# Moving row moments from VectorE to ScalarE in a Mamba and linear-attention kernel, with a fourth x buffer and a reordered end

## What is computed

```
# block 1: conditional Mamba, state size N = 16, inner width 512
xn = layernorm(x) * (1 + scale) + shift          # scale, shift, gate from cond
x_in, z = split(xn @ in_proj.T)
u  = silu(causal_conv4(x_in) + conv_b)
dt_r, B, C = split(u @ x_proj.T);  dt = softplus(dt_r @ dt_proj.T + b)
h[t] = exp(dt[t] * A) * h[t-1] + dt[t] * u[t] * B[t]       # 512 x 16 states
y = (h . C + u * D) * silu(z)
x = x + gate * (y @ out_proj.T)
# block 2: linear attention, 8 heads of 32
xn = layernorm(x);  q = softmax(xn Wq, in a head);  k = softmax(xn Wk + mask, over rows)
v = (xn Wv) * mask;  y = q @ (k^T v)
x = x + silu(layernorm(y) * (1 + scale2) + shift2) @ W_out
```

## Time and profile before

| | us |
|---|---|
| median of 3 runs | 567.08 |
| lowest, highest | 566.95, 568.99 |
| the profiled execution, its own time | 567.71 |
| its span in the profile | 565.9 |

### The profile page before, as it was taken

The page is one execution under the profiler, slowest core; times in us unless marked ns, Lnnn a source line. Parts: engine busy times, 40 slices in busy tenths (PEclk is TensorE's granted clock), DMA queues, the critical chain, the costliest instruction groups (busy, mean ns, idle before and its releaser), DMA issues. The chain is left out here.

```text
span 565.9 us, 7375 instructions
## 1 busy us (share of the span) xinstructions
PE 437.7 (77%) x2448; PEld 361.3 (64%) x2448; DVE 515.5 (91%) x567; ACT 407.9 (72%) x896; POOL 452.8 (80%) x318
## 2 busy tenths in 40 slices
PE   8968656769787878859787688759787877766887
PEld 7647445557675767638675567647585766655776
DVE  2489999999999999999999999999999999999753
ACT  2693868588857989498947989489857988486533
POOL 4058979988997999978996989878996989995121
PEclk8978868888789899998879898999789798889899
DMA  8293043003320145012320045012330044000001
GB/s 255 80 346 109 0 151 113 37 28 107 103 92 0 30 158 161 1 29 87 139 94 1 28 152 167 1 30 78 124 118 1 10 152 167 2 0 20 0 1 37
DMA packets 22365, 45.37 MB, mean 80 GB/s; under 512 B 3684, under 2 KB 13556, under 8 KB 22328
## 3 DMA queue, kind: packets, MB, share of 16 engines
q1 hardware_dynamic: 22328, 44.92, 24.2%
HBM read 42.52 MB, written 2.39 MB: 79 GB/s over the span
## 5 line engine op out<-in xcount | busy, mean ns | idle before, releaser
L531 POOL TENSOR_TENSOR hs<-dtu,Br 128x1024 f32<-128x1024 f32 x127 | 296.8, 2359 | 7.9 <-DMA Br<-bc_rows 6.4
L726 ACT ACTIVATE ring<-dt,Aneg 128x256 f32<-128x256 f32 x512 | 212.9, 465 | 71.9 <-DVE hs L965 67.4
L958 DVE TENSOR_TENSOR_SCAN ring<-ring,hs 128x1024 f32<-128x1024 f32 x97 | 221.4, 2282 | 4.3 <-ACT ring L726 4.0
L1317 PE MATMUL sums<-ident,hs 128*128 128x128 f32 x1024 | 148.7, 301 | 37.8 <-DVE hs L965 37.7
L1317 PEld LDWEIGHTS sums<-ident,hs 128*128 128x128 f32 x1024 | 132.7, 157 | 49.0 <-DVE hs L965 45.5
L965 DVE TENSOR_TENSOR hs<-ring,Cr 128x1024 f32<-128x1024 f32 x97 | 118.7, 1224 | 3.3
L540 POOL TENSOR_TENSOR hs<-hs,Cr 128x1024 f32<-128x1024 f32 x31 | 73.1, 2357 | 39.8 <-DVE hs L958 39.8
L958 DVE TENSOR_TENSOR_SCAN hs<-ring,hs 128x1024 f32<-128x1024 f32 x31 | 70.3, 2268 | 0.0
L1385 PE MATMUL PY<-wqkvo,xT 128*128 128x256 f32 x168 | 49.8, 450 | 0.0
L1385 PEld LDWEIGHTS PY<-wqkvo,xT 128*128 128x128 f32 x168 | 39.9, 237 | 7.7
L616 ACT ACTIVATE conv<-PX,par 128x256 f32<-128x256 f32 x28 | 14.3, 559 | 38.2 <-PE PX L1251 38.0
(11 more groups left out here) (221 smaller groups left out, 693.6 us busy)
## 6 DMA issues: line engine op xcount, KB each, us to landing
Br<-bc_rows SPq DMA_DIRECT2D x32, 512.0 KB, 5.2
Cr<-bc_rows SPq DMA_DIRECT2D x32, 512.0 KB, 4.2
xg<-in_x SPq DMA_DIRECT2D x8, 256.0 KB, 2.9
out<-fin SPq DMA_DIRECT2D x7, 256.0 KB, 4.3
hs<-in_ada_wT SPq DMA_DIRECT2D x3, 512.0 KB, 5.2
win<-in_in_wT SPq DMA_DIRECT2D x2, 512.0 KB, 7.2
hs<-in_W_emb SPq DMA_DIRECT2D x2, 512.0 KB
gate<-gate_rows SPq DMA_DIRECT2D x8, 128.0 KB, 3.1
```

The costliest lines, as they stand in the source:

```text
L531: nc.gpsimd.tensor_tensor(hs[:, g % DBUF], dtu[:, b % 2, dc, :].unsqueeze(1).to_broadcast([P, NQ, T]), Br[:, NQ * q:NQ * q + NQ, :], ALU.m ...
L726: ins = nc.scalar.activation(ring[:, g % 2, j, :], dt[:, b % 2, dc, :], ACT.Exp, scale=Aneg[:, c:c + 1])
L958: V.tensor_tensor_scan(driven if by_pool(g) else decays, decays, driven, 0.0, ALU.mult, ALU.add).then_inc(s_scan_done, 1)
L1317: ins = M(YT[:, c, :], hs[:, g % DBUF, j, P * c:P * c + P], ident[:, :], is_transpose=True, start=False, stop=(q == UPC - 1 and j == NQ - ...
```

## The change

Five edits.
1. `moments` on ACT takes the place of `stats` on DVE for x of batches 2 to 7 and for the attention's rows of batches 0 to 5: two Copy ACTIVATEs with an accumulator (the negative mean), then, behind a wait for these, two Square ACTIVATEs with the bias from them (the sum of squared deviations). Their elementwise output goes into `xhat` or `xh` and is not used. POOL's `rstd` then has three operations instead of four for these.
2. `moments2` stands first among the steps behind unit 2, `moments0` last among those behind unit 3 (slot -29, four units ahead of where `stats0` stood).
3. `normalize2` moves from behind unit 6 to behind unit 4, POOL's `rstd2` by one unit.
4. XBUF is 4; x of batch 3 is loaded right behind x of batch 2 at the start, and each later load is that of one batch later, at the same place in SP's queue and behind the same wait.
5. The end: the last unit's product with C is made in two halves; `last_early` is split, its second half now ahead of unit 126's sums; ACT does `exp_k` of the last batch ahead of `normalize2` of batch 6, and the last `silu_h` ahead of `finish` of batch 6; PE's transposes of the last batch's rows come ahead of the addition of x1 for batch 6, and ten `keep_on` matmuls are gone.

```diff
-DBUF, XBUF = 10, 3
+DBUF, XBUF = 10, 4
+def moments_by_act(which, b):
+    return b >= 2 and which == 0 or b < LAST_B - 1 and which == 2
...
             load_x(2)
+            load_x(3)
...
-                if b + 2 < NB:
-                    load_x(b + 2)
+                if b + 3 < NB:
+                    load_x(b + 3)
...
+                if summed:
+                    nc.gpsimd.tensor_scalar(ve[:, :], mv[:, :, 1], 1.0 / D, EPS, ALU.mult, ALU.add).then_inc(ve_sem, 1)
...
+                if summed:
+                    nc.gpsimd.tensor_tensor(nb[:, :], mv[:, :, 0], rs[:, :], ALU.mult).then_inc(rs_sem, 1)
+                    return
...
-                                   (40, rstd2)):
+                                   (39, rstd2)):
...
+            def moments(b, src, junk, mv, ready):
+                for c in range(TC):
+                    nc.scalar.activation(junk[:, c, :], src[:, c, :], ACT.Copy, scale=-1.0 / D,
+                                         accum_out=mv[:, c, 0:1]).then_inc(ready, 1)
+                for c in range(TC):
+                    act.wait_ge(ready, 2 * TC * b + TC)
+                    nc.scalar.activation(junk[:, c, :], src[:, c, :], ACT.Square, bias=mv[:, c, 0:1],
+                                         accum_out=mv[:, c, 1:2]).then_inc(ready, 1)
+            def moments0(b):
+                if not moments_by_act(0, b):
+                    return
+                act.wait_ge(x_loaded[b % XBUF], 16 * (b // XBUF + 1))
+                act.wait_ge(s_xT_mm, b)
+                act.wait_ge(s_rs0_ready, 2 * b)
+                moments(b, xg[:, b % XBUF], xhat, mv0, s_st0_ready)
+            def moments2(b):
+                if not moments_by_act(2, b):
+                    return
+                act.wait_ge(s_yq_ready, b + 1)
+                act.wait_ge(s_x1T_mm, b + 1)
+                act.wait_ge(s_rs2_ready, 2 * b)
+                moments(b, yq, xh, mv2, s_st2_ready)
...
+                exp_k(LAST_B)
                 normalize2(LAST_B - 1)
-                exp_k(LAST_B)
...
+                silu_h(LAST_B)
                 finish(LAST_B - 1)
-                silu_h(LAST_B)
...
-                for slot, step in ((-17, normalize0), ...
+                for slot, step in ((34, moments2), (-17, normalize0), ...
-                                   (33, copy_kT), (38, normalize2), (42, finish)):
+                                   (33, copy_kT), (36, normalize2), (42, finish), (-29, moments0)):
...
+                if g == NB * U - 1:
+                    for half, done in ((slice(0, 2), s_last_half), (slice(2, NQ), s_hc_dve)):
+                        V.tensor_tensor(hs[:, g % DBUF, half], ring[:, g % 2, half], Cr[:, NQ * q:NQ * q + NQ, :][:, half],
+                                        ALU.mult).then_inc(done, 1)
+                    return
...
-                output(b - 1)
-                keep_on(4)
+                output_rows(b - 1)
                 pe.wait_ge(s_yh_ready, TC * b + 1)
                 turn_half(z, xhat, 0)
                 pe.wait_ge(s_yh_ready, TC * b + 2)
                 turn_half(z, xhat, 1).then_inc(s_yT_mm, 1)
+                output_x1(b - 1)
...
-                keep_on(6)
...
+                if g == LAST_B * U + 13:
+                    last_early(1)
                 if g == LAST_B * U + 14:
-                    last_early()
+                    last_early(0)
```

More of the change, by code:

```diff
@@ L477, in _, with rstd @@
             pool.wait_ge(s_pool_const, 8)
-            def rstd(ready, b, mv, ve, rs, nb, ve_sem, rs_sem, nbp_sem):
+            def rstd(which, ready, b, mv, ve, rs, nb, ve_sem, rs_sem, nbp_sem):
                 pool.wait_ge(ready, 2 * TC * (b + 1))
-                nc.gpsimd.tensor_scalar(ve[:, :], mv[:, :, 1], EPS, None, ALU.add).then_inc(ve_sem, 1)
+                summed = moments_by_act(which, b)
+                if summed:
+                    nc.gpsimd.tensor_scalar(ve[:, :], mv[:, :, 1], 1.0 / D, EPS, ALU.mult, ALU.add).then_inc(ve_sem, 1)
+                else:
+                    nc.gpsimd.tensor_scalar(ve[:, :], mv[:, :, 1], EPS, None, ALU.add).then_inc(ve_sem, 1)
                 pool.wait_ge(ve_sem, b + 1)
@@ L485, in rstd @@
                 pool.wait_ge(rs_sem, 2 * b + 1)
+                if summed:
+                    nc.gpsimd.tensor_tensor(nb[:, :], mv[:, :, 0], rs[:, :], ALU.mult).then_inc(rs_sem, 1)
+                    return
                 nc.gpsimd.tensor_tensor(nb[:, :], mv[:, :, 0], rs[:, :], ALU.mult).then_inc(nbp_sem, 1)
-                pool.wait_ge(nbp_sem, b + 1)
+                pool.wait_ge(nbp_sem, sum(not moments_by_act(which, c) for c in range(b + 1)))
                 nc.gpsimd.tensor_scalar(nb[:, :], nb[:, :], -1.0, None, ALU.mult).then_inc(rs_sem, 1)
@@ L492, in rstd0 @@
                     pool.wait_ge(s_xhat_ready, TC * b)
-                rstd(s_st0_ready, b, mv0, ve0, rs0, nb0, s_ve0_ready, s_rs0_ready, s_nbp0)
+                rstd(0, s_st0_ready, b, mv0, ve0, rs0, nb0, s_ve0_ready, s_rs0_ready, s_nbp0)
             def softplus_sum(b, h):
@@ L549, in rstd1 @@
                     pool.wait_ge(s_xh_ready, TC * b)
-                rstd(s_st1_ready, b, mv1, ve1, rs1, nb1, s_ve1_ready, s_rs1_ready, s_nbp1)
+                rstd(1, s_st1_ready, b, mv1, ve1, rs1, nb1, s_ve1_ready, s_rs1_ready, s_nbp1)
             def rstd2(b):
@@ L554, in rstd2 @@
                     pool.wait_ge(s_yh_ready, TC * b)
[L555 removed]
+                rstd(2, s_st2_ready, b, mv2, ve2, rs2, nb2, s_ve2_ready, s_rs2_ready, s_nbp2)
             for g in range(FIRST, LAST):
@@ L1315, in sum_states @@
                 for j in range(NQ):
+                    if g == NB * U - 1 and j == 2:
+                        pe.wait_ge(s_hc_dve, dve_units(g + 1))
                     for c in range(TC):
@@ L1359, in out_part, with last_early @@
                 return ins
-            def last_early():
+            def last_early(c):
                 pe.wait_ge(s_last_yg, 3)
-                for c in range(TC):
-                    out_part(c, (0, 1, 2))
+                out_part(c, (0, 1, 2))
             def out_half(dst, c):
```

15 lines of the change are left out of this document (13 added, 2 removed).

## The result

| | before | after |
|---|---|---|
| median of 4 runs each | 567.72 us (566.95 to 568.99) | 559.74 us (558.04 to 560.05) |
| profiled execution | 567.7 us, span 565.9 | 559.8 us, span 558.0 |
| mean granted clock of PE | 0.897 | 0.887 |

The ratio is 0.9852, 95% interval 0.9835 to 0.9869: 8.0 us less. 557.4 was forecast, with 554.5 to 562.0 as its range; it was reckoned from the 567.08 of the three runs known then, and from 567.72 the same 9.7 us would give 558.0. The change took 7.9 us from the span; the steps had promised 9.7.

The account below looks back on a forecast made before the run. DVE, busy 515.5 of 565.9 us, was taken as the bound, with ACT possibly late next. Gains of 4.8 + 3.5 - 0.6 + 2.0 = 9.7 us from the median of 567.1 gave 557.4 us, range 554.5 to 562.

Parts of the forecast that it names:

- The set on ACT: One set of moments on ACT, two Copies and two Squares: 2.0 us, between 1.8 and 2.6.
- DVE's busy time: Sign over the whole kernel: DVE busy 12 us less, about 503.5 us.
- A: Attention's moments moved from DVE to ACT, units 34 to 114: most of each 1.0 us set kept, 4.8 us gained.
- B: x's moments on ACT and normalize2 moved: 0.5 us at each of five places, 1.0 behind unit 23; 3.5 us gained.
- C: First moments0, behind unit 3, waits for x of batch 2 and delays the decays of unit 4: 0.6 us lost.
- D: The end: split product and last_early 0.15 us, exp_k first 0.75, last transposes ahead of x1's addition 1.1; 2.0 us gained.
- milder form of rival 1: PE's half clock falls elsewhere and delays ACT's convolution tap more often, at 0.2 to 0.5 us each.
- a new wait of DVE for PE: Sign named in advance: if such a wait appeared, the prediction would be wrong.
- Rival 1: ACT is late in most stretches, with a set of 2.6 us: 562.2 us; chance 0.2 for 560.5 to 564.
- Rival 2: Slower: a set keeps ACT over 3.2 us, where all 9.7 us are gone; 569.5 at 3.5; chance 0.04.
- Rival 3: The end keeps its time, PE falling to half clock without the ten dummies: 559.9 us; chance 0.07.
- Rival 4: No change within 0.5%: ACT's chain absorbs both sets and the end gives 2, about 565 us; chance 0.05.

Follow-up runs that it names:

- Run 8: The change with 16 spare PE matmuls per batch 2 to 7, every set of moments on ScalarE done twice: 575.59 us, ratio 1.0134.
- Run 1: The change with normalize2 put back to slot 38 and rstd2 to slot 40: 559.94 us, ratio 0.9861.
- run 6: The change with 16 spare PE matmuls per batch 2 to 7, x's moments on VectorE again, only the attention's on ScalarE: 558.92 us, ratio 0.9830.
- run 12: The change with 26 spare PE matmuls ahead of the sums of unit 6 in batches 2 to 7: 556.02 us, ratio 0.9787.
- run 3: The change with all moments of batches 0 to 7 on VectorE again, the rest kept: 569.05 us, ratio 1.0022.
- run 9: The change itself measured again, unaltered, on one chip beside later runs: 559.15 us, ratio 0.9829.
- run 2: The change with 16 spare PE matmuls ahead of the sums of unit 6 in batches 2 to 7: 556.89 us, ratio 0.9809.
- run 4: The change with the diff of the end reversed, so the old end: 559.27 us, ratio 0.9861.
- run 5: The kernel before with 16 spare PE matmuls ahead of the sums of unit 6 in batches 2 to 7: 568.14 us, ratio 1.0010.

## Why the prediction was right, and which terms were off

The direction, the mechanism and the size held: 559.7 us against 557.4, inside the range, though 2.3 us on the slow side. By its own steps:

- **The set on ACT** was sized at 2.0 us from `exp_k`'s row; it is 1.94: 0.40 us for each Copy, 0.50 for each Square and 0.12 for the wait between them. By the formula of the Trainium skill ("ScalarE: Activation LUTs", What ACT_TABLE_LOAD costs), with 0.1 us for each accumulator read, my estimate had been 1.8; the trace agrees with it to 0.01 us for each of the four, and only the wait was missing. (Run 8's added set, without wait and bias, takes 1.61 us.)
- **DVE's busy time** was forecast at 503.5 us and is 504.7.
- **A**, 4.8 us, came to 8.1. The steady steps are 0.94 us at unit 51 and 83 and 0.66 at 115 (0.9 or 0.65, and 0.7 forecast). The other three came to 1.37, 2.68 and 1.47, because in the kernel before ACT's tap had waited 6.51, 8.00 and 6.50 us for PE there, against 5.11 elsewhere, and DVE's taps had waited behind it for 0.33, 1.66 and 0.43 us. The largest, in the timeline of DVE before:

```profile
298.30 2.43 DVE L920 SCALAR_TENSOR_TENSOR conv<-PX,par,conv 128x255 f32<-128x255 f32 x6 [1.66 <-ACT conv L616]
```

  From 290 to 295 us the granted clock was 0.50 there. In the changed kernel ACT's tap waits for PE in none of these batches. I had taken the before profile's bad spots for fixed and priced them as a loss for the change ("0.65 kept"), where they were a gain.
- **B**, 3.5 us: 0.94 and 5 x 0.45 = 3.2. Run 1 and run 6 confirm it from two sides: normalize2 back costs 0.45 at each place; with x's set on DVE the waits at unit 8 go.
- **C**, -0.6 us: the set did wait (5.46 us, for the load), the decays ended at 51.01 us, 0.5 after the old scan's start. But DVE had been 0.5 us behind since unit 2, ahead of this set, and at unit 9 the difference was gone; I did not look for the reason. Worth 0 here, and 0.2 at most in the other profiles (a wait of 0.17 us at unit 4 in run 12), near the better of my bounds.
- **D**, 2.0 us: 1.75 in the parts that I had priced at 0.75 and 1.1 (from kmax to vm 4.95 us before, 4.22 after, 0.73; the rest is behind it). The split of the last product and `last_early`, priced at 0.15, shows nothing beyond the spread of the middle column (6.92 to 7.24 with the old end; 6.97 to 7.33 with the new, but 6.56 in the change and 7.9 in runs 3 and 8).
- **What was missing.** The sum had no term for the clock. It stood only as the milder form of rival 1 ("PE's half clock falls elsewhere"), at 0.2 to 0.5 us a time; it is 1.6 to 1.7 us a time, three times in the first profile and once in run 9's. I had written that a new wait of DVE for PE would prove me wrong: it appeared (2.31 us at unit 113, against 0.57 before), and it comes at a granted clock of 0.50 to 0.55 (from 470 to 480 us). The move of normalize2, which step B counts as a gain of 2.5 us, also joins idle pieces of PE. That this joining causes the losses at unit 11 of a batch is supported by runs 1 and 2; the one at unit 113 stands some 35 us behind the joined piece of batch 6 and is gone in runs 1, 2, 4 and 9 alike, so its own cause is not shown beyond the low clock. So the total came out near the forecast in part by luck: A gave 3.3 us more than its term, D and C together about 1, and some 6 us of losses had no term at all. In run 2 the body is 488.7 us, 9.9 below the profile of before, where A, B and C had promised 7.7; most of the difference is the three waits under A, 2.4 us in all.
- **Rival 1** (ACT late in most stretches) did not come true: a set of 1.94 us just fits, and the decays of unit 4 of a batch are late by 0.2 us at most in the change. Its milder form, with PE's clock, did. **Rival 2** (slower) had its place right and its point too high: run 8's slope is 0.97 us for each us of ScalarE, 11.6 us for each us that a set is longer, so by a straight line a gain of 8 us would be gone at an estimated 1.94 + 8/11.6 = 2.6 us, not at 3.2; no run has such a set. Only there would ScalarE be the wrong place for the sums. **Rival 3** is refuted: from 545 us on the windows show 1.00 with and without the dummies, and the last column is 1.75 us shorter with the new end each time. **Rival 4** is refuted by the ratio.

Not tried: moving x_proj ahead of `output` on PE, filling the idle piece of 3 to 4 us around unit 12 of each batch, and the fourth x buffer alone.

## What to carry to other kernels

When a step moves on an engine that is not the bound, look at what its removal does to the idle pieces of the engine that waited for it: here, with one piece of 3.7 us in place of 2.0 to 2.4 and 1.7, PE's clock was low behind it in six batches instead of one or two, and spare work in that piece gave back about 2 us, on another engine and some 15 us further on. When medians differ by under 1%, split the span into parts that start and end at the same instruction and compare those: the end's 1.75 us repeats to 0.02 us while the total hides it (run 4). And before an expected loss is fixed, double its supposed cause: run 8 took one run to show that the wait at unit 8 does not depend on how long the moments keep ScalarE.

## What was not expected of the hardware

- A kernel's execution on one core scatters by some 4 us (558.36 to 562.54 us in run 4, 555.19 to 558.60 in run 2; the kernel before ran once in 563.57 us beside run 5, where its other twelve runs took 566.80 to 569.96). Much of it lies in where PE's clock is low: the change and run 9 have the same program, the first scan starts at 31.95 and 33.18 us, and the long waits stand at units 43, 107 and 113 in one and at 91 in the other.
- With 16 matmuls of 97x256 in bf16, 1.9 us, in PE's idle piece of batch 2, the granted clock behind it was 1.00, against 0.50 without them; in batch 6 it was 0.50 without, 0.81 with 16 and 1.00 with 26 (3.0 us where they were recorded at full clock).
- ScalarE's accumulating ACTIVATE of 128x256 from SBUF had a pitch of 0.40 us for Copy (0.50 for Square with a bias from SBUF), its accumulator read of 186 ns hidden but for 0.1 us; the step from the second Copy to the first Square, which waits for the sums, adds 0.12 us.
